# Second attention of a four-layer block: when four normalizing operations and two context loads are issued

## What is computed

```python
x = x + _L0_xattn_ref(ctx_1024, _layernorm(x), ...)     # phase A
x = x + _L0_ffn_ref(_layernorm(x), ...)                 # phase B, experts
x = x + _L1_xattn_ref(ctx_1024, _layernorm(x), Wq, Wk, Wv, 1, 0, 1)   # phase C
x = x + _L1_ffn_ref(_layernorm(x), ...)                 # phase D, experts
```

```python
q = _split_heads(_layernorm(x) @ Wq.T, 8)      # 8 heads of 32
k = _split_heads(ctx_1024 @ Wk.T, 8)
v = _split_heads(ctx_1024 @ Wv.T, 8)
attn = softmax(einsum('bhnd,bhmd->bhnm', q, k) * 32 ** -0.5)
x = x + einsum('bhnm,bhmd->bhnd', attn, v)     # heads side by side again
```

## Time and profile before

| what | value |
|---|---|
| median of 3 runs (lowest, highest) | 2724.38 us (2721.0, 2725.88) |
| the profiled execution: its time, its span | 2723.15 us, 2721.6 us |
| busy in the span: PE, DVE, ACT, POOL | 91%, 69%, 62%, 60% |
| mean granted clock of PE | 0.958 |
| second attention | about 1762 to 2375 us of the span |

### The profile page before, as it was taken

How to read it: one execution, slowest core, us unless ns; L and a number is a source line. 1 busy time by engine, 2 the same in 40 slices (tenths; PEclk the granted TensorE clock), 3 DMA queues, 4 the chain that set the end, 5 groups by cost and what they waited for, 6 DMA issues and landing times. The chain is left out here.

```text
span 2721.6 us, 46305 instructions
## 1 busy us (share of the span) xinstructions
PE 2477.8 (91%) x15187; PEld 1489.6 (55%) x15314; DVE 1865.4 (69%) x3467; ACT 1675.5 (62%) x2694; POOL 1636.6 (60%) x1442
## 2 busy tenths in 40 slices
PE   4999999999999999999999389867999999869997
PEld 2455555555555555555554268734555554447886
DVE  5678767787777786777676565347787888677443
ACT  3465665556655566555555375436787878758664
POOL 3467766677667676656567244416676769825443
PEclk9999999999999999999999589979999999969999
DMA  3000000000000000000000383231111101076223
GB/s 117 25 1 1 4 22 1 1 1 1 25 1 1 1 1 1 1 1 1 1 1 0 112 243 78 41 101 40 32 41 26 48 19 30 3 215 188 46 46 66
DMA packets 88377, 107.92 MB, mean 40 GB/s; under 512 B 16322, under 2 KB 77715, under 8 KB 88163
## 3 DMA queue, kind: packets, MB, share of 16 engines
q1 hardware_dynamic: 67140, 76.37, 9.3%
q0 software_dynamic: 19200, 24.97, 5.7%
q10 hardware_dynamic: 1856, 4.19, 0.4%
HBM read 68.75 MB, written 25.88 MB: 35 GB/s over the span
## 5 line engine op out<-in xcount | busy, mean ns | idle before, releaser
L396 POOL TENSOR_TENSOR a_acc<-a_acc,a_pf 128x512 f32<-128x512 f32 (+1 forms) x480 | 645.3, 1344 | 388.0 <-ACT a_pf L524 367.8
L1993 POOL TENSOR_TENSOR c_pl<-c_pf,c_ph 128x512 f16<-128x512 f32 x320 | 378.3, 1210 | 169.0 <-ACT c_ph L2092 168.7
L524 ACT ACTIVATE a_pf<-a_psS 128x1024 f32<-128x1024 f32 (+1 forms) x288 | 281.2, 976 | 303.8 <-PE a_psS L663 300.2
L813 DVE TENSOR_TENSOR a_pl<-a_pf,a_ph 128x512 f16<-128x512 f32 x448 | 405.4, 914 | 28.2 <-ACT a_ph L530 28.2
L789 DVE TENSOR_REDUCE a_mx<-a_psA 128x1 f32<-128x512 f32 x512 | 344.9, 685 | 48.8 <-PE a_psA L600 42.6
L530 ACT ACTIVATE a_ph<-a_psS 128x1024 f16<-128x1024 f32 (+1 forms) x288 | 281.0, 976 | 0.0
L1303 POOL DMA_INDIRECT f_sums<-f_xn,f_sidx x78 | 138.9, 1781 | 228.1 <-DVE f_xn L1668 191.6
L2324 DVE TENSOR_REDUCE c_mx<-c_psA 128x1 f32<-128x512 f32 x384 | 251.0, 685 | 34.4 <-PE c_psA L2163 32.4
L2085 ACT ACTIVATE c_pf<-c_psS 128x1024 f32<-128x1024 f32 x192 | 197.7, 1030 | 89.4 <-PE c_psS L2197 88.5
L784 DVE TENSOR_TENSOR a_vl<-a_psA,a_vh 128x256 f16<-128x256 f32 (+1 forms) x272 | 115.2, 423 | 167.2 <-ACT a_vh L469 164.3
L1162 DVE TENSOR_TENSOR f_xn<-f_xn 128x256 f16<-128x256 f32 x312 | 129.6, 424 | 127.8 <-ACT f_xn L1133 123.5
(11 more groups left out here) (329 smaller groups left out, 6382.8 us busy)
## 6 DMA issues: line engine op xcount, KB each, us to landing
f_stage<-in_L_ffn_w SPq DMA_DIRECT2D x16, 1024.0 KB, 5.6
f_stage<-in_L_ffn_W SPq DMA_DIRECT2D x16, 1024.0 KB, 5.3
c_kst<-c_khs SPq DMA_DIRECT2D x64, 100.1 KB, 2.2
a_cx<-in_ctx SPq DMA_DIRECT2D x4, 1536.0 KB
c_cx<-in_ctx SPq DMA_DIRECT2D x12, 512.0 KB, 4.1
f_xrow<-f_xn SPq DMA_DIRECT2D x8, 512.0 KB, 3.2
f_sums<-X SPq DMA_DIRECT2D x2, 2048.0 KB, 12.4
c_kst<-c_kls SPq DMA_DIRECT2D x32, 100.1 KB, 2.2
```

The source lines that it names most:

```text
L396: g.tensor_tensor(acc[0:k, p, :], acc[0:k, p, :], pf[0:k, q % RF, i, :], ALU.add).then_inc(s_acc, 1)
L524: act.activation(pf[0:r, q % RF, 0:k, :], psS[q % 2][0:r, 0:k, :], ACT.Exp, scale=SCALE).then_inc(s_pF, 1)
L813: v.tensor_tensor(pl[0:r, q % RP, i, :], pf[0:r, q % RF, i, :], ph[0:r, q % RP, i, :], ALU.subtract).then_inc(s_pL, 1)
L1993: g.tensor_tensor(pl[0:r, q % RP, i, :], pf[0:r, q % RF, i, :], ph[0:r, q % RP, i, :], ALU.subtract).then_inc(s_pG, 1)
```

## The change

`norm` takes a range of row tiles. The four operations of "nx" stand one each at the end of units 1, 2, 3 and 4 of head 3, where all four stood at the end of unit 2. SP issues the loads of chunks 0 and 1 of the next batch ahead of a batch's stacking, where they stood behind it. No instruction is added or removed.

```diff
     NORMED = {"xs": ST, "xa": 2 * ST, "nx": 3 * ST}
-    NORM_AT = {(2, 0): "xs", (2, 2): "xa", (3, 2): "nx"}
+    NORM_AT = {(2, 0): ("xs", 0, ST), (2, 2): ("xa", 0, ST)}
+    NORM_AT.update({(3, 1 + i): ("nx", i, i + 1) for i in range(ST)})
...
             for b in range(B):
-                for c in range(NK):
+
+                for c in range(0 if b == 0 else 2, NK):
                     load_context(b, c)
...
+                if b + 1 < B:
+                    for c in range(2):
+                        load_context(b + 1, c)
                 stack(b)
...
-            def norm(b, kind):
+            def norm(b, kind, lo=0, hi=ST):
                 if kind == "xa":
                     v.wait_ge(s_st, 3 * ST * b + NORMED["xs"])
-                elif kind == "nx":
+                elif kind == "nx" and lo == 0:
                     v.wait_ge(s_rstd, b + 1)
...
-                for u in range(ST):
+                for u in range(lo, hi):
...
-                        norm(b + 1, NORM_AT[h, u])
+                        norm(b + 1, *NORM_AT[h, u])
```

## The result

The changed kernel took 2702.49 us in the median (four executions, 2696.61 to 2703.08) against 2724.02 (2721.0 to 2725.88) for the kernel before, run beside it. The ratio is 0.9917 with a 95% interval of 0.9900 to 0.9934, or 22.6 us less (18.0 to 27.2); the two medians themselves lie 21.5 us apart. The profiled execution took 2703.08 us, with a span of 2701.5 instead of 2721.6. The forecast was 2700 with a range of 2690 to 2711.

A forecast was written before the change was run, and what follows sets the result against it. TensorE, the busiest engine, was taken to lose time standing still or at its lower clock. 9.5 us for the load plus 3 x 4.8 for the operations gave 23.9 off 2723.15, said as 2700 us, range 2690 to 2711.

The forecast's parts named there:

- The load: Context loads of the first batch, issued ahead of the stacking: 9.5 us gained (bounds 8.6 to 10.3); later batches 0.
- correction of 0.8 us: First batch's key product: ACT begins its exponential some 0.8 us later than in steady heads, taken off a 10.3 us gain.
- The walk through head 3: Spread operations in head 3: one 3.25 us PE wait becomes 0.9, 0.2 and 1.8; value product 1.2 us sooner.
- A batch without a fall: Head 3 with PE's clock staying at full: 3.55 + 1.7 - 0.4 = 4.8 us gained for a batch.
- The 0.4 I had put on operation 3: Last normalizing operation, before the last maximum of head 3: estimated to cost 0.4 us of waits.
- The clock: PE's clock in head 3: stays at full in most batches; if it falls, a batch gains only 0.5 to 1.2 us.
- Rival 1: Head 3: close waits make the clock fall after all; a batch gives 1.2 us, time 2710; chance 0.20.
- the case named under rival 1: Head 3: the clock falls in one batch of three; time 2703 us; no chance of its own given.
- Rival 2: Head 3: the operations hide fully, POOL idle or VectorE's gaps taking them; 7.9 us a batch, time 2690; chance 0.16.
- Rivals 3 and 4: 3: moved load gives nothing, 2709, chance 0.05. 4: four waits hold head 3's clock at half, 2743, chance 0.03.

## Why the prediction was right

The load: forecast 9.5, measured 9.44 in the profile of the whole change, and 10.1 (6.5 to 13.3) with the loads alone. The stacking was not delayed, and a correction of 0.8 us to the 10.3 of the steady heads was about right (0.9 measured); that ACT's lag is the whole of it is argued and not tested. With the loads alone the second and third batches were 0.35 and 0.2 us shorter than before, where the forecast had 0; that is too little to tell from where the low stretch lay against the wait.

The walk through head 3: forecast waits of 0.9, 0.2 and 1.8 us and a value product 1.2 us sooner; measured 0.80, none, 1.78, and 1.19. The operations were put at 1.03, 0.5, 1.1 and something between 0.25 and 1.2, and took 1.06, 0.56, 1.22 and 0.40. That an operation lasts until POOL's current one ends, plus 0.15 us, and takes at least 0.40 (not the 0.25 that I had taken as the least), is what the rows before and after show; the four in a row that take 2.28 us where POOL is mostly idle, instead of 3.81, show it from the other side. The Trainium skill (SBUF — State Buffer, Who interferes with whom) has the same rule, and the trace agrees: each operation that met POOL at work ends 0.15 us behind POOL's, or after its own 0.40. Left out of the estimate for the four behind the copy, it made that one 1.2 us a batch too pessimistic.

A batch without a fall: forecast 4.8, measured 5.2 and 5.5. The 0.4 I had put on operation 3 did not appear; POOL was idle when it began.

The clock: here the forecast was right in total partly by luck, since two errors went opposite ways. I took "stays at full" as likeliest for most batches and, for a fall, a gain of only 1.2, as if the low stretch kept its 9.5 us. The clock fell in 11 of 15 batches, so falls are the rule with these two waits; but the low stretches were 3.4 or 6.8 us, and such a batch still gains 3.6 or 1.9, above the 0.5 to 1.2 of my bounds. Rival 1's mechanism is real and its price was too high. With one fall of 6.8 us in the profiled execution the sum is 9.4 + 5.5 + 1.9 + 5.2 = 22.0, which lies between the forecast's 23.9 and rival 1's 13.1. It is nearest to the case named under rival 1, a fall in one batch of three, at 2703. The Trainium skill (TensorE: Matmul & The Clock Gate, Part 4: PE-mode transpose) says that transposes do not count as PE being busy as matmuls do. No run here shows whether this bears on the falls: the transposes stand between the two waits in the changed kernel, where the clock fell, and just the same with two operations ahead of the copy, where it did not, and none took them away.

Rival 2 (all hidden, 7.9 us a batch) was right only for operation 3, and came nearly true where the operations were put behind the copy: a batch of 133.2 us with the four together gives 6.9, one of 132.3 with the four apart gives 7.8. Rivals 3 and 4 did not occur. What stays open is what decides, from one execution to the next, in which batches the clock falls and for how long: the waits are the same to 0.01 us. Nor was it tested whether the length of the second wait decides or that of the two together.

## What to carry to other kernels

Spreading small operations helps only as far as they leave the stretch that another engine waits on: count what still stands ahead of that wait, not how many are together. Here four in a row behind the copy did better than one each, three of them ahead of it. A transfer whose only condition is a free buffer belongs ahead, in an in-order issue queue, of a long group with later conditions: here one chunk's load so moved was worth some 9.4 us.

When two waits of PE come close together, price the clock separately, and take a profile several times before reading its clock: one execution shows one pattern.

## What was not expected of the hardware

The granted clock fell behind a pair of waits of 0.80 and 1.78 us with 2.9 us of matmuls and transposes between them, in 11 of 15 batches, and in none behind 0.80 and 0.62 (3 batches) or 0.38 and 0.77 (6 batches). The low stretches behind these waits came in three lengths, 3.4 us, 6.8 us and, with the single wait of 3.25 us, 10.2 us (6 of 6), and nothing between.

The same tensor_scalar of 128x256 fp32 took 0.40 us with POOL idle and up to 1.25 with POOL at work. A bad place costs three times a good one.
